# A recommendation tower on one core: first layer of the last two tiles in fp32 products, and one more embedding of that round fetched by comparing

## What is computed

```python
e = jnp.stack([tbl_0[ids[:, 0]], tbl_1[ids[:, 1]], ..., tbl_25[ids[:, 25]]], axis=1)
combined = jnp.concatenate([dense[:, None, :], e], axis=1)          # 2048 x 27 x 128
inter = jnp.einsum('bnd,bmd->bnm', combined, combined)[:, TRIU_I, TRIU_J]
h = jnp.concatenate([dense, inter, dense], axis=1)                  # 2048 x 607
h = jnp.maximum(h @ W_top1 + b_top1, 0.0)                           # 512
h = jnp.maximum(h @ W_top2 + b_top2, 0.0)                           # 256
y = h @ W_top3                                                      # 1
```

## Time and profile before

| | us |
|---|---|
| median of 3 runs (lowest, highest) | 472.18 (470.95, 473.91) |
| profiled execution, whole | 471.37 |
| its span in the trace | 469.5 |
| outside of the span | 1.87 |
| busy in the span: PE, DVE, ACT, POOL | 417.1, 338.4, 223.7, 396.2 |

### The profile page before, as it was taken

How to read it: one execution, slowest core, us unless ns; L and a number is a source line. 1 busy time by engine, 2 the same in 40 slices (tenths; PEclk the granted TensorE clock), 3 DMA queues, 4 the chain that set the end, 5 groups by cost and what they waited for, 6 DMA issues and landing times.

```text
span 469.5 us, 11728 instructions
## 1 busy us (share of the span) xinstructions
PE 417.1 (89%) x4210; PEld 392.8 (84%) x4210; DVE 338.4 (72%) x777; ACT 223.7 (48%) x727; POOL 396.2 (84%) x553
## 2 busy tenths in 40 slices
PE   0766969989999989998799969999699988999898
PEld 0766869889999979898798969999698978988786
DVE  5897897986888677885597657876678855956260
ACT  3853654536553535455254443545254552536152
POOL 7899999899989998998998998899899899899600
PEclk9988997999999989999899999999899998999999
DMA  7992225122212312231212312222122212121100
GB/s 213 263 227 83 78 80 168 51 75 77 78 44 79 83 39 86 74 82 43 80 45 74 87 40 80 51 77 74 45 82 74 83 43 80 41 80 41 35 2 0
DMA packets 20046, 36.82 MB, mean 78 GB/s; under 512 B 8109, under 2 KB 10677, under 8 KB 19994
## 3 DMA queue, kind: packets, MB, share of 16 engines
q0 software_dynamic: 8704, 17.84, 14.3%
q1 hardware_dynamic: 11290, 18.28, 13.7%
HBM read 36.09 MB, written 0.01 MB: 77 GB/s over the span
## 4 chain that ended last, share of the span: by engine, by line
POOL 55%; issue 28%; PE 6%; DMA 3%; ACT 3%; DVE 2%; SPq 1%; POOLq 1%; DVEq 0%; ACTq 0%
POOL rows L414 29%; POOL y_wide L403 25%; DMA vecs<-in_tbl 3%; PE turn_ps L489 2%; PE dots_ps L473 1%; DVE inter L889 1%; POOLq L402 1%; ACT dots_ps L686 1%; SPq L297 1%; PE turn_ps L554 1%; PE mlp_ps L563 1%; DVE onehot L836 1%; ACT t_hi L679 1%; PE dots_ps L554 1%; DVE t_lo L853 1%
## 5 line engine op out<-in xcount | busy, mean ns | idle before, releaser
L414 POOL DMA_INDIRECT rows<-in_tbl,idx_sb x272 | 261.9, 963 | 45.6 <-POOL y_wide L403 43.7
L836 DVE TENSOR_TENSOR onehot<-ids_sb,late_ps 125x1024 fp32r<-125x1024 int32 (+2 forms) x154 | 167.3, 1143 | 8.2 <-DMA ids_sb<-in_ids_by_round 4.5
L889 DVE COPY_PREDICATED inter<-mask,dots_ps 27x48 f32<-27x48 int32 x496 | 103.1, 208 | 63.0 <-ACT inter L703 44.2
L403 POOL MEMSET y_wide<- 64x448 f32 x272 | 134.2, 493 | 0.2
L703 ACT COPY inter<-dots_ps 27x64 f32<-27x64 f32 x496 | 99.4, 200 | 67.0 <-PE dots_ps L473 54.5
L473 PE MATMUL dots_ps<-vecs 128*64 128x54 f32 x1984 | 117.3, 224 | 1.5 <-ACT vecs L672 0.9
L473 PEld LDWEIGHTS dots_ps<-vecs 128*64 128x64 f32 x1984 | 113.3, 139 | 5.8 <-issue 2.1
L489 PE MATMUL turn_ps<-onehot,t_hi 125*128 125x256 f32 x378 | 103.6, 309 | 13.6 <-DVE vecs L652 10.3
L489 PE MATMUL turn_ps<-onehot,t_lo 125*128 125x256 f32 x378 | 98.3, 295 | 0.0
L489 PEld LDWEIGHTS turn_ps<-onehot,t_hi 125*128 125x128 f32 x378 | 77.5, 205 | 18.5 <-issue 8.5
L489 PEld LDWEIGHTS turn_ps<-onehot,t_lo 125*128 125x128 f32 x378 | 77.5, 205 | 0.2
(11 more groups left out here) (86 smaller groups left out, 371.8 us busy)
## 6 DMA issues: line engine op xcount, KB each, us to landing
ids_sb<-in_ids_by_round SPq DMA_DIRECT2D x25, 384.0 KB
rows<-in_tbl,idx_sb POOLq DMA_INDIRECT x272
vecs<-in_tbl SPq DMA_DIRECT2D x8, 448.0 KB
rows<-in_r_dense_features SPq DMA_DIRECT2D x16, 64.0 KB
h_sb<-in_W_top_laid SPq DMA_DIRECT2D x2, 512.0 KB
vecs<-in_tbl SPq DMA_DIRECT2D x1, 560.0 KB
w_sb<-in_W_top SPq DMA_DIRECT2D x1, 512.0 KB
vecs<-in_tbl SPq DMA_DIRECT2D x8, 52.0 KB
```

Of the source, the lines that this page charges most:

```text
L403: pool.memset(unread, 0.0).then_inc(pauses_made, 1)
L414: nc.gpsimd.indirect_dma_start(out=rows[v % 2][:, s, :], out_offset=None, in_=tables[f - 1][:, :], in_offset=bass.IndirectOffsetOnAxis(ap= ...
L836: dve.tensor_tensor(part_buffer(k, h)[0:KP, 0:n], home.rearrange("p (o r) -> p o r", o=1).to_broadcast([KP, n, R]), row_of[KT[k]][0:KP, a: ...
L889: dve.copy_predicated(inter_of(u, q, g, a, n), mask[g * 32:g * 32 + N, a:a + n].rearrange("p (j s) -> p j s", s=1).to_broadcast([N, n, QS] ...
```

## The change

1. In the last round, embedding 25 is no longer gathered (one gather and one memset fewer for each of tiles 14 and 15). Its table is loaded into the space of `t_lo` (`t_added`), split by ACT and DVE in step 6, compared by DVE (`compare_added`) and fetched by PE at the start of the last step (`fetch_added`, 20 matmuls).
2. Layer 1 of tiles 14 and 15 goes by tiles and without rounding: `inter` itself is the moving operand of fp32 matmuls with w_hi and w_lo (`end_layer1`), 40 matmuls a tile. Tile 14's stand where `stay_busy` stood; tile 15's are done unit by unit, 40 matmuls of 64 columns each. Layers 2 and 3 of the two tiles are separate. `split_input` of both tiles goes, `place_dense` (one ACT copy) comes.
3. In steps 3 to 6, items 3 and 4 are fetched before the rows of groups 2 to 4 of the odd tile, and compared before the merge ahead of them.
4. The queues of SyncE and of the last four tiles on POOL are written out.

The diff, cut to what the following speaks of:

```diff
+            def load_added(i):
...
+                sp.wait_ge(onehot_used, halves_made(i, 0, 2))
+                src = tables[ADDED - 1].rearrange("(p t) d -> p (t d)", t=LONG)
+                for a, b in ((0, 112), (112, KP)):
+                    sp.dma_start(t_added[a:b], src[a:b]).then_inc(added_in, 16)
...
-                turns += [("item", n + 1, 1), ("item", n + 1, 2), *(("rows", 2 * n + 1, k) for k in range(NG))]
+                turns += [("item", n + 1, 1), ("item", n + 1, 2), ("rows", 2 * n + 1, 0), ("rows", 2 * n + 1, 1)]
+                if n >= FROM:
+                    turns += [("item", n + 1, 3), ("item", n + 1, 4)]
+                turns += [("rows", 2 * n + 1, k) for k in range(2, NG)]
...
+        def gathered_of(tile, k):
+
+            return [s for s in groups[k] if tile not in LAST_TILES or ORDER[s] != ADDED]
...
                 pool.sem_inc(tiles_begun, 1)
                 for k, group in enumerate(groups):
                     for s in group:
-                        if ORDER[s]:
+                        if ORDER[s] and not (static(i) and s not in gathered_of(i * 4 + v, k)):
...
+            def end_layer1(i, v, u, bank_of_part, *ms):
+
+
+                cols = slice(0, P) if u is None else slice(u * (P // UNITS), (u + 1) * (P // UNITS))
+                units = v * UNITS + (UNITS if u is None else u + 1)
+                pe.wait_ge(inter_by_act, i * (4 * NA) + units * PER_UNIT)
+                pe.wait_ge(inter_by_dve, i * (4 * ND) + units * PER_UNIT)
+                pe.wait_ge(x_hi_made, i * 8 + 4 + v - 1)
+                for m in ms:
+                    for w in (w_hi, w_lo):
+                        for jj in range(JG + 1):
+                            last = pe.matmul(bank_of_part(m)[:, cols], w[:, jj, m * P:(m + 1) * P].bitcast(F32),
+                                             inter[:, jj, cols] if jj < JG else end_dense[:, v - 2, cols],
+                                             start=(w is w_hi and jj == 0), stop=(w is w_lo and jj == JG))
+                    if u != 0:
+                        last.then_inc(h1_done, 1)
+
+            def end_layer2(i, v, banks):
+                before = i * (2 * M1) + M1 + (v - 2) * M1
+                mine = slice((v - 2) * P, (v - 1) * P)
+                for ks in (range(M1 - 1), (M1 - 1,)) if v == 3 else (range(M1),):
                     for m in range(M2):
                         for k in ks:
                             pe.wait_ge(relu1_done, before + k + 1)
-                            last = pe.matmul(mlp_ps[m], w2_sb[:, k, m * P:(m + 1) * P], h1_sb[:, k, :],
+                            last = pe.matmul(banks[m], w2_sb[:, k, m * P:(m + 1) * P], end_h1_sb[:, k, mine],
                                              start=(k == 0), stop=(k == M1 - 1))
                         if M1 - 1 in ks:
                             last.then_inc(h2_done, 1)
+
+            def end_layer3(i, v):
+                mine = slice((v - 2) * P, (v - 1) * P)
                 for k in range(M2):
-                    pe.wait_ge(relu2_done, i * (2 * M2) + M2 + k + 1)
-                    last = pe.matmul(end_ps[0][0:1], w3_sb[:, k:k + 1], end_h2_sb[:, k, :],
+                    pe.wait_ge(relu2_done, i * (2 * M2) + M2 + (v - 2) * M2 + k + 1)
+                    last = pe.matmul(mlp_ps[1][0:1, mine], w3_sb[:, k:k + 1], end_h2_sb[:, k, mine],
                                      start=(k == 0), stop=(k == M2 - 1))
-                last.then_inc(y_done, 1)
+                if v == 3:
+                    last.then_inc(y_done, 1)
+
+            def end_of_layers(i):
+                end_layer1(i, 3, 0, lambda m: end_ps[m], *range(M1))
+
+                pe.wait_ge(y_kept, i * 2 + 1)
+                end_layer2(i, 2, end_h2_ps[0])
+                end_layer1(i, 3, 1, lambda m: end_ps[m], *range(M1))
+                end_layer3(i, 2)
+                end_layer2(i, 3, end_h2_ps[1])
+                end_layer3(i, 3)
...
+                if soon(i, r):
+                    fetch(i, r, 3)
+                    fetch(i, r, 4)
                 transpose_rows(i, v + 1, (2, 3, 4))
-                fetch(i, r, 3)
+                if not soon(i, r):
+                    fetch(i, r, 3)
                 dots(i, v + 1, 0)
-                fetch(i, r, 4)
+                if not soon(i, r):
+                    fetch(i, r, 4)
...
             def last_step(i):
                 transpose_rows(i, 2, range(NG))
+                fetch_added(i)
                 layer1(i, 0, 0)
                 dots(i, 2, 0)
                 layer1(i, 0, 1, 2)
@@ -633,21 +708,23 @@
                 layer1(i, 0, 3)
                 transpose_rows(i, 3, (2,))
                 layer2(i, 0, 0)
-
-                stay_busy(row_ps, 32)
+                layer2(i, 0, 1)
+
+                end_layer1(i, 2, None, lambda m: end_first_ps[m], 0, 1)
                 transpose_rows(i, 3, (3,))
-                layer2(i, 0, 1)
-                stay_busy(row_ps, 4)
+                layer3(i, 0)
+                end_layer1(i, 2, None, lambda m: end_first_ps[m], 2, 3)
                 transpose_rows(i, 3, (4,))
                 dots(i, 3, 0)
+
+                pe.wait_ge(relu1_done, i * (2 * M1) + 2 * M1)
                 dots(i, 3, 1, last_dots_ps)
-                layer3(i, 0)
                 end_of_layers(i)
...
+
+            def place_dense(i, v):
+
+                act.wait_ge(*taken(turn_of["rows", i * 4 + v, 0]))
+                nc.scalar.copy(end_dense[:, v - 2, :].rearrange("p (h two s) -> p h two s", two=2, s=QS),
+                               in_turn(vecs[1][:, v - 2, :, 0])).then_inc(x_hi_made, 1)
...
+                if now == (PASSES - 1, 0):
+                    split(N_PIECES)
                 split_input(i, v)
+                if soon(i, r):
+                    copy_fetched(i, r, 3, 4)
...
             def last_step(i):
                 take_vectors(i, 2, 0, 2, 4)
+                copy_added(i)
                 rectify1(i, 0, 0)
                 take_products(i, 2, 0)
                 rectify1(i, 0, 1, 2)
                 take_products(i, 2, 1)
                 take_vectors(i, 3, 1)
+                place_dense(i, 2)
                 rectify1(i, 0, 3)
-                split_input(i, 2)
-
-                act.wait_ge(*taken(turn_of["rows", i * 4 + 3, 0]))
-                split_dense(i, 3)
+                rectify2(i, 0, 0, 1)
                 take_vectors(i, 3, 3)
-                rectify2(i, 0, 0, 1)
+                place_dense(i, 3)
+                end_rectify1(i, 2, lambda m: end_first_ps[m])
                 take_products(i, 3, 0)
                 take_products(i, 3, 1, last_dots_ps)
-                split_input(i, 3, False)
-                for m in range(M1):
-                    act.wait_ge(h1_done, i * (2 * M1) + M1 + m + 1)
-                    nc.scalar.activation(h1_sb[:, m, :], end_ps[m], ACT.Relu, bias=b1_sb[:, m:m + 1]).then_inc(relu1_done, 1)
-                for m in range(M2):
-                    act.wait_ge(h2_done, i * (2 * M2) + M2 + m + 1)
-                    nc.scalar.activation(end_h2_sb[:, m, :], mlp_ps[m], ACT.Relu,
-                                         bias=b2_sb[:, m:m + 1]).then_inc(relu2_done, 1)
+                end_rectify2(i, 2, end_h2_ps[0])
+                end_rectify1(i, 3, lambda m: end_ps[m])
+                end_rectify2(i, 3, end_h2_ps[1])
 
...
+                if soon(i, r):
+                    compare(i, r, 4)
...
+                if now == (PASSES - 1, 0):
+                    split(N_PIECES)
...
+                if now == (PASSES - 1, 0):
+                    compare_added(i)
+                else:
+                    compare(i, r, 9)
...
@@ -970,14 +1088,11 @@
                 merge_products(i, 2, 0)
                 merge_products(i, 2, 1)
                 take_vectors(i, 3, 0, 2)
-                split_input(i, 2)
-                split_dense(i, 3)
+                keep_y(i, 0)
                 take_vectors(i, 3, 4)
                 merge_products(i, 3, 0)
                 merge_products(i, 3, 1, last_dots_ps)
-                keep_y(i, 0)
-                split_input(i, 3, False)
-                keep_y(i, 1, end_ps[0])
+                keep_y(i, 1, mlp_ps[1])
```

More of the change, by code:

```diff
@@ L115, in dlrm_tower @@
         t_hi = sb("t_hi", [P, T0[X], D], F32R)
+        with nc.sbuf_tensor("t_added", [P, LONG * D], F32) as t_added:
+            pass
         t_lo = sb("t_lo", [P, T0[X], D], F32R)
@@ L163, in dlrm_tower @@
         assert M1 == len(end_ps)
-        end_h2_sb = rows[0][:, 0:M2 * R // D, :].rearrange("p s d -> p (s d)").rearrange("p (m r) -> p m r", r=R)
+        end_first_ps = [row_ps[:, m * P:(m + 1) * P] for m in range(M1)]
+        end_h2_ps = [[mlp_ps[0][:, 0:P], mlp_ps[0][:, P:2 * P]], [mlp_ps[0][:, 0:P], row_ps[:, 0:P]]]
+        end_h1_sb, end_dense, end_h2_sb = [
+            rows[0][:, a:b, :].rearrange("p s d -> p (s d)").rearrange("p (m r) -> p m r", r=r)
```

(47 more changed lines are left out.)

122 lines of the change are left out of this document (68 added, 54 removed).

## The result

| | before | after |
|---|---|---|
| median of 4 runs each (lowest, highest), us | 471.56 (470.27, 473.91) | 485.15 (484.18, 487.51) |
| ratio, 95% interval | | 1.029 (1.0233 to 1.0347) |
| profiled execution, whole; span | 471.37; 469.5 | 487.51; 485.7 |

The kernel is 2.9% slower. The forecast was 483.8 and slower; the range of 474.5 to 488.5 holds the median. The profiled execution of after is the slowest of its four, 2.4 over their median.

What follows compares the result with a forecast made beforehand. Gathers bound the kernel up to the last at 441.39, then a 23 us tail; with PE late, 449.2 + 7.15 + 21.65 + 3.1 = 481.1, plus 1.87 outside and 0.8 to the median: 483.8, range 474.5 to 488.5.

Steps and rivals of the forecast that it cites:

- (c): Start of last step: fetch_added's 20 matmuls take 2.4 us; layer 1 of the round before starts at 418.0 (417.6 to 418.9).
- (d): Last step: the unchanged 16.0 us end at 434.0, group 2's rows take 0.5, layer 2 3.5, reaching 438.0.
- (e): Tile 14's layer 1, 9.0 us, leaves PE 7.5 later than the gathers; dots of tile 15 start at 449.2, not 444.99.
- (f): Tile 15: unit 0 merged 7.15 us after dots start, then 21.65 of PE work without a gap.
- (a): POOL's queue: two gathers fewer, tile 15's last issued 3.2 us earlier, worth 3.2 if nothing else were late.
- (b): Items 3 and 4 fill tile 13's waits, some 5 us a step, returning at the next even tile; covers embedding 25's table.
- third rival: Embedding 25's table load lands late and holds up the step; last step up to 3 us later, 487; chance 0.10.
- (g): Kernel's end: from layer 2's first ReLU to the end takes 3.1 us in place of 3.7.
- the 0.11 for 64 columns: Expected sign in the changed profile: layer 1 records of 64 moving columns start 0.11 us apart, as those of 128 do.
- Moving columns set the price: Rival on tile 15's layer 1: 64-column records cost 0.056 us, each half 4.5; median 475.2, no measurable change; chance 0.13.
- One record for each product: Rival: rounded weights make each fp32 matmul one record, halving all three layer 1 passes; median 470.5; chance 0.07.
- 6 us of slack: PE's spare time before the second-last and last groups of the last step, some 6 us, to take up the added work.

Runs made afterwards that it cites:

- e3_products_only: Changed kernel with embedding 25 gathered to the end and items 3 and 4 back in place, leaving only the fp32 products by tiles: 483.85 us, ratio to before 1.0257.
- e1_one_pass: Changed kernel with tile 15's layer 1 run once over 128 columns, after both units are merged, instead of twice over 64: 478.06 us, ratio to before 1.014.
- e5_price: Changed kernel with most products of tile 15's layer 1 cut: unit 0 to 64 weight columns, unit 1 to 32 moving columns: 487.07 us, single run.
- e2_rounded_end: Changed kernel with the rounded F32R layer 1 of the last two tiles back, without unread transposes in the waits: 469.61 us, ratio to before 0.997.
- e6_rounded_no_items: Kernel before with only embedding 25 fetched by comparing, rounded end, no unread transposes, items 3 and 4 where they were: 469.54 us, ratio 0.9957.
- e8_filled: e7_added_ahead with layer 2 ahead of tile 15's waits for groups 3 and 4, and unread transposes in them: 468.28 us, ratio to before 0.9949.
- e4_items_only: Changed kernel with embedding 25 gathered and the rounded end as before; items 3 and 4 ahead and written-out queues stay: 471.42 us, ratio to before 0.9996.
- e7_added_ahead: e2_rounded_end with fetch_added, and ACT's copy of its result, moved ahead of tile 14's groups 3 and 4: 470.75 us, ratio to before 0.9977.

## Why the prediction was right

Its main statement holds: the fp32 records cost by their weight columns, only the slack of PE takes them up, and PE becomes what is late. e3_products_only shows that the products carry the loss; e1_one_pass and e5_price show that half the moving columns cost as much, and that fewer weight columns cost less. That the weight load is what takes this time fits its rows, but was not varied by itself. By its steps:

| step | forecast | after | e1_one_pass |
|---|---|---|---|
| (c) layer 1 of the round before starts | 418.0 (417.6 to 418.9) | 420.49 | 419.39 |
| (d) layer 2 starts | 434.5 | 438.49 | 436.57 |
| (e) tile 14's layer 1, in two parts | 9.0 | 9.0 | |
| (f) `dots` to unit 0 | 7.15 | 7.01 | |
| (f) unit 0, layer 2, unit 1 | 8.8, 1.8, 8.8 | 8.98, 1.84, 8.98 | |
| `dots` to the end of the span | 31.9 | 32.4 | |

(The forecast of (d) is its 434.0 and the rows' 0.5; the 31.9 are 7.15 + 21.65 + 3.1.)

- **(a)** Right. The last gather is issued at 438.32 and 438.17 in e1_one_pass and e2_rounded_end, 3.1 and 3.2 earlier than before (after's own at 439.45, 1.9 earlier). The gain shows only where PE isn't late, and is 0.3 to 0.5% there (e2_rounded_end, e6_rounded_no_items, e8_filled).
- **(b)** Right that the items bring nothing and that the wait comes back at the next even tile (e4_items_only). Wrong that they fill both waits of tile 13: that for group 4 stays, 2.27 in e4_items_only and 1.18 in e1_one_pass. Wrong too that the split of embedding 25's table is covered by the time won. In step 6 it stands on DVE ahead of the copy of tile 13's last rows:

```profile
391.27 1.48 DVE L968 TENSOR_TENSOR t_lo<-t_added,t_hi 125x1280 fp32r<-125x1280 f32 x1
392.67 0.41 DVE L729 COPY vecs<-turn_ps 128x256 f32<-128x256 f32 x1
...
413.86 3.00 DVE L951 TENSOR_TENSOR onehot<-ids_sb,late_ps 125x768 fp32r<-125x768 int32 x4
...
417.12 1.27 DVE L729 COPY vecs<-turn_ps 128x512 f32<-128x512 f32 x2
```

  The 1.48 at 391.27 stand between the rest of tile 12 and that copy, and `dots` of tile 13, which need it, waited 2.75 before 393.19 and then ran at a granted clock of 0.67, 5.18 for the first half. In e1_one_pass they waited 1.51 and ran at 1.00, 3.65, and PE later waited for tile 14's gathers (1.08 and 1.33) all the same, so that nothing was lost there. In after the loss counts, and it was the second of its kind. PE's timeline shows both:

```profile
363.92 0.59 PE L495 MATMUL turn_ps<-ident,rows 128*128 128x128 f32 x2 [2.16 <-DMA rows<-in_tbl,idx_sb]
...
393.19 5.25 PE L519 MATMUL dots_ps<-vecs 128*64 128x54 f32 x64 [2.75 <-issue]
```

  At tile 12's last group, where before did not wait, the gather issued at 360.24 took 3.63 to land. PE waited 2.16 for it and ran the next 15 products at a granted clock of 0.52, in 3.43 (0.73, 1.00 and 1.96 in e1_one_pass). So PE came to tile 14's rows at 414.91, and in e1_one_pass at 410.92. The split is the third rival's mechanism, though not its cause: ACT began the rounding of the table at 385.81, next to the instruction ahead of it, so the load was not what it waited for.
- **(c)** The step that was mis-sized. It said that "DVE's four comparisons replace two that nobody used and end before". In after's profiled execution they do not: the 3.00 at 413.86 stand ahead of tile 14's copies at 417.12, PE waited 0.99 for a bank of the transposes, and layer 1 started 2.5 later than forecast. The rest of the 2.5 is PE's late arrival under (b), which held up DVE too: in e1_one_pass the same compares began at 410.17. There PE did not wait for DVE, and layer 1 started at 419.39 by the half clock that (c) had as its upper case: the 20 records took 3.7, behind tile 14's last gather.
- **(d)** Right in its lengths, but layer 2 does not follow group 2 at once. It waits for ACT's last ReLU of layer 1, 1.65 here and 0.58 in e1_one_pass:

```profile
437.08 0.59 ACT L729 COPY vecs<-turn_ps 128x512 f32<-128x512 f32 x1
437.56 0.41 ACT L797 COPY rows<-vecs 128x128 f32<-128x128 f32 x1
437.87 0.48 ACT L820 ACTIVATE h_sb<-mlp_ps,small 128x256 f32<-128x256 f32 x1
```

  The ReLU (L820) comes after the products of tile 14, a copy of rows (L729) and the new `place_dense` (L797). Before, layer 2 did not wait there: from group 2 at 434.29 to the filler at 436.51 is just room for four transposes and its eight records. Now each such wait is time at the end.
- **(e), (f), (g)** Right. The two half passes cost 0.36 more than forecast together, what follows them 0.2 more, and unit 0 starts 0.14 sooner behind `dots`: the 0.5 between 31.9 and 32.4.

Of the signs that the prediction named, the 0.11 for 64 columns came, and neither of the two against its mechanism did: PE waited neither for tile 15's last gather nor for the merge ahead of unit 1. But PE did not stand without a wait from 415 on; it waited 0.99, 1.65 and 0.51.

*Moving columns set the price* fell: 0.111 at 128, 64 and 32 moving columns, for 128 weight columns. *One record for each product* fell: each pass shows 80 records in the timeline (x8 and x2 in turn, four times for each weight). The start of `dots` was 4.1 later than forecast in the profiled execution and 2.2 later in e1_one_pass, by (c) and (d); the median was 1.35 over the forecast. A part of that closeness is luck: the forecast adds 0.8 because the profiled execution of before lay so far under a median of three, and with the four of the result it lies 0.2 under (471.37 and 471.56). With 0.2 the forecast would have been 2.0 too low. What delayed the executions without a trace is open.

Three readings in the prediction are off, without weight for its sum. PE is late by 7.7, not 7.5 (448.4 less 440.7). Of the 6 us of slack, 0.92 stands before the third-last group and not before the last two. And the load rows, less the 82 ns, lie within 3 ns of the 53 and 107 named under e5_price, not within 2.

## What to carry to other kernels

Splitting a matmul's moving columns to start earlier doubles its price where the weight columns set it, as here (0.111 us a record at 128, 64 and 32 moving columns); look at the distance of two starts in the nearest stream, for the same weight columns, before counting on half. Work put into an engine's waiting time is free up to the slack, which is read from the timeline of the last step and not from the busy share; from there on, each wait of that engine for a small copy or ReLU is added at the end. And a wait taken away may come back one place later with a half clock behind it: fill it, or look where it goes.

## What the runs showed that was not expected

- The granted clock fell to 0.56 while PE issued records without a gap, 128 weight columns with mostly 32 moving (e5_price). With 64 moving columns, as in after, it stayed at 1.00 through both units. Which quantity the clock follows was not tested further.
- At the half clock (0.50 from 471.60 to 473.30 in e5_price), eight records of 128 weight and 32 moving columns took 1.70 in place of 0.89, so what sets their price runs with the same clock.
- The same eight records of layer 2 took 1.7 where PE had worked ahead of them without a wait (e2_rounded_end) and 3.4 behind a wait of 4.28 (e7_added_ahead). With unread transposes in the waits, and layer 2 ahead of them, the granted clock stayed at 1.00 (e8_filled).
- Waiting cost twice in step 6 of after: the wait, and then the clock. After 2.16 and 2.75 the next work ran at 0.52 and 0.67 of full speed, and each time took 1.5 us more than the same work at 1.00 in e1_one_pass.
